# The loop over the batches of an attention and expert block: 28 passes of an engine loop written out as straight code

## The reference, cut to what matters

```python
x = L0_attn_x                                  # [32, 512, 256]
mod = (_silu(L0_c) @ L0_wmod).reshape(32, 6, 1, -1)
sa, ca, ga, sb, cb, gb = (mod[:, n] for n in range(6))
# ga, gb: pushed away from zero to at least 0.25 in size
h = _layernorm(x) * (1 + ca) + sa
x = x + ga * attention(h, w_qkv, b_qkv, w_out, b_out)
#   scores = q.k / 4 + alibi_causal_mask; probs = softmax(scores); out = probs.v @ w_out.T + b_out
h = _layernorm(x) * (1 + cb) + sb
x = x + gb * experts(h, gate_W, expert_W, out_W)
#   p = softmax(h @ gate_W.T); cnt[e] = how many entries of (p > 0.3) equal e; out = sum_e cnt[e] p[e] (h @ expert_W[e].T) @ out_W.T
```

## Time and profile before

| what | us |
|---|---|
| median of 3 runs | 1957.47 |
| fastest and slowest of them | 1957.25, 1957.89 |
| span of the profiled execution, first to last instruction | 1953.2 |
| TensorE busy in it | 1724.6 (88%) |
| VectorE busy | 1552.6 (79%) |
| ScalarE busy | 1214.8 (62%) |
| GpSimd busy | 998.9 (51%) |

### The profile page before, as it was taken

One profiled execution on the slowest core, in us unless ns is written; L12 is line 12 of the kernel. 1 busy time (PEld: TensorE's weight loads), 2 busy tenths in 40 slices (PEclk: granted clock), 3 DMA queues, 4 the chain that ended last, 5 costly groups with the idle time before them and its releaser, 6 DMA issues.

```text
span 1953.2 us, 62334 instructions
## 1 busy us (share of the span) xinstructions
PE 1724.6 (88%) x17744; PEld 995.6 (51%) x17744; DVE 1552.6 (79%) x5632; ACT 1214.8 (62%) x2466; POOL 998.9 (51%) x1225
## 2 busy tenths in 40 slices
PE   5799999998989998999999898999899999999974
PEld 3455555555555455555555555545555555555542
DVE  5778888888888878888888888887888888888843
ACT  1366666666666666666666666666666666666651
POOL 3234555545545455555554554545555545455454
PEclk8799999999999999999999999999999999999986
DMA  4243333433333443333344333344333334433321
GB/s 131 77 133 116 125 119 128 141 128 124 125 104 125 140 136 126 120 125 120 128 141 128 123 125 104 126 141 136 125 120 125 121 129 139 131 123 115 120 88 45
DMA packets 206753, 238.21 MB, mean 122 GB/s; under 512 B 27626, under 2 KB 153138, under 8 KB 206674
## 3 DMA queue, kind: packets, MB, share of 16 engines
q1 hardware_dynamic: 206710, 237.67, 37.3%
HBM read 135.13 MB, written 101.81 MB: 121 GB/s over the span
## 4 chain that ended last, share of the span: by engine, by line
PE 49%; DVE 24%; issue 18%; ACT 4%; DMA 2%; DVEq 2%; POOL 1%; SPq 1%; ACTq 0%; POOLq 0%
PE ps L497 18%; PE ps L589 12%; DVE ps L853 9%; PE ps L575 8%; PE ps L609 4%; PE ps L603 4%; DVE mxt L853 4%; DVE ol L868 2%; DVEq L257 1%; ACT hf_a L658 1%; ACT hh_a L660 1%; DVE qk_st L793 1%; DVE st_c L759 1%; ACT prob L647 1%; PE ps L515 1%
## 5 line engine op out<-in xcount | busy, mean ns | idle before, releaser
L853 DVE CUSTOM_DVE_ANT_0 ps<-ps,mask_qk 128x512 f32<-128x512 f32 (+3 forms) x2048 | 971.1, 510 | 296.3 <-PE ps L589 285.3
L647 ACT ACTIVATE prob<-ps 128x512 f32<-128x512 f32 (+1 forms) x1536 | 743.5, 530 | 363.2 <-PE ps L575 362.3
L589 PE MATMUL ps<-kz,qs 112*128 112x512 f16 (+3 forms) x2048 | 542.4, 307 | 138.2 <-DVE mxt L853 129.5
L1018 POOL TENSOR_SCALAR_AFFINE_SELECT prob<-prob 128x512 f32<-128x512 f32 x512 | 353.4, 696 | 364.2 <-ACT prob L647 364.2
L575 PE MATMUL ps<-qs,kz 114*128 114x128 f16 (+2 forms) x3584 | 453.3, 243 | 3.7 <-DMA qs<-negm 3.1
L589 PEld LDWEIGHTS ps<-kz,qs 112*128 112x128 f16 x2048 | 187.1, 97 | 492.8 <-DVE mxt L853 308.6
L853 DVE DVE_READ_ACCUMULATOR2_ANT mxt<- 128x1 f32 x2048 | 288.6, 141 | 0.0
L575 PEld LDWEIGHTS ps<-qs,kz 114*128 114x128 f16 x3584 | 259.7, 98 | 50.5 <-ACT prob L647 3.8
L609 PE MATMUL ps<-prob,va 128*32 128x384 f32 (+2 forms) x3072 | 237.0, 380 | 0.0
L603 PE MATMUL ps<-prob,va 128*32 128x128 f32 x4096 | 218.3, 285 | 2.0 <-issue 0.9
L679 ACT ACTIVATE qk_st<-ps,bqk 128x512 f16<-128x512 f32 x128 | 88.0, 688 | 97.7 <-PE ps L497 95.7
(11 more groups left out here) (115 smaller groups left out, 2818.7 us busy)
## 6 DMA issues: line engine op xcount, KB each, us to landing
qk_d<-qk_st SPq DMA_DIRECT2D x128, 256.0 KB, 2.0
ou_d<-ou SPq DMA_DIRECT2D x128, 256.0 KB, 2.0
qs<-qk_d SPq DMA_DIRECT2D x128, 192.0 KB, 2.6
kz<-qk_d SPq DMA_DIRECT2D x256, 96.0 KB, 2.6
xa<-in_L_attn_x SPq DMA_DIRECT2D x32, 512.0 KB, 4.3
qk_d<-qk_st SPq DMA_DIRECT2D x128, 128.0 KB, 1.9
xc<-in_L_attn_x SPq DMA_DIRECT2D x32, 512.0 KB, 3.5
oc<-ou_d SPq DMA_DIRECT2D x64, 256.0 KB
```

Source lines behind the costliest of these rows:

```text
L589: x_ = mm(ps[:, bank, col:col + w], qs[0:CONST, h // 2, qt * P:(qt + 1) * P], kz[0:CONST, h, 0:w], start=True, stop=True)
L647: nc.scalar.activation(prob[:, h % 8, at:at + w], ps[:, ST + n, 0:w], ACT.Exp, scale=1.0 / FS).then_inc(s["exp_done"], 1)
L853: x_ = v.tensor_tensor_reduce(ps[:, bank, col:col + w], ps[:, bank, col:col + w], mask_qk[:, S - w:S], 1.0, -3e38, ALU.add, ALU.max, mxt[: ...
L1018: q.affine_select(out=d, in_=d, compare_op=ALU.is_ge, fill=0.0, base=0, pattern=[[0, 4], [1, P]], channel_multiplier=-1).then_inc(s["maske ...
```

## The change

The loop on the engines goes. All 36 iterations are written out with a plain number for i. The order of the work on each engine, the tiles, the tables and the transfers stay.

```diff
         def iterations(eng, one, first=-2):
 
-            for i in range(first, 2):
-                one(i)
-            with eng.Fori(2, NB - 2) as i:
-                one(i)
-            for i in range(NB - 2, NB + 2):
+            for i in range(first, NB + 2):
                 one(i)
```

## The result

The changed kernel took **1899.04 us** (median of 4, 1897.75 to 1901.19), the kernel before 1957.36 beside it; the ratio is 0.970, interval 0.969 to 0.972. The direction was forecast, the size was not: 1923 was said, and 1906 as the low end. The gain is 58 us in place of 34.

What follows compares the result with a forecast made beforehand. TensorE was taken as the bound, waiting 5.2 us per iteration, mostly for VectorE's row maxima. 0.91 + 0.32 = 1.23 us over 28 iterations gave 34.4 us off, hence 1923 us; range 1906 to 1940, 8 in 10.

Steps and rivals of the forecast that it cites:

- The bound and the mechanism: TensorE bounds while fed; its waits for VectorE's maxima shrink as each real hand-over gets 0.16 us shorter, 0.58 to 0.42.
- That hit was on one of the worst places: Late store in iteration 30, delaying the negated maxima, TensorE waiting 0.30 us in slot 8; its net gain taken as mean.
- The 0.91 us: Gain per iteration from head to end of TensorE's longest wait, 45.80 us in iteration 29 against 44.89 in iteration 30.
- The first term: Stretch from iteration head to end of TensorE's longest wait in slot 12: gain of 0.91 us per iteration.
- the second: Rest of the iteration behind the longest wait: 0.92 us less in iteration 30, of which 0.32 credited to the change.
- Iteration 30's missing batch: No batch 32 to load and normalise in iteration 30; the 0.60 us wait behind the statistics was credited to that.
- The low end: Lower end of the 8 in 10 range, 1906 us, the time of the rival giving all 1.83 us to the change.
- Rival 1: Missing statistics cost iteration 30 nothing, so all 1.83 us is the change's: 28 x 1.83 = 51.2, 1906 us; chance 0.12.
- worth of 8 of them: Size check: 1.23 us per iteration equals 8 hand-overs at 0.16 us less each; not a further term.
- Rival 2: Instruction blocks delay transfers more on average than in iteration 30: 1949 us, or 1932 with only 0.32 lost; chance 0.23.
- Rival 3: TensorE runs out of instructions, up to 1.25 us per late block: 2011 us with one in two late; chance 0.05.
- Rival 4: No difference: a wait for DMA in slot 8 or ScalarE takes back the cheaper hand-over, 1957 us; chance 0.05.

Runs made afterwards that it cites:

- e1: All engines written out except TensorE, which keeps the loop of 28 passes: 1880.31 us, ratio 0.960 to the kernel before.

## Why the prediction was wrong

**The bound and the mechanism** were right. TensorE does the same matmuls, and its waits shrank; the hand-over went from 0.58 to 0.42 us as read from the one straight iteration, and putting the increment back brought 0.58 and 36 us. TensorE's own register work and its branch were costed at nothing, and e1 shows it. The clock stayed (a mean of 0.977 to 0.980 in the runs of the kernel before, 0.976 to 0.977 in those of the changed kernel).

**The step that failed** is the one that said of the delayed transfer "That hit was on one of the worst places, so I keep the net figure as the mean over the 28 iterations". The 0.91 us was net of what the late store cost iteration 30, and I had priced that from the one wait marked DMA, 0.30 us. Its true price is seen by iteration 30 of the changed kernel, the same instructions and work: up to the end of the long wait of slot 12 it takes 43.36 us against 44.89, 1.53 less. By slots, 0.91 of it lies in slots 6 to 8 (11.82 against 10.91), 0.34 in the start behind the loop's last pass (2.30 against 2.14 up to the first maximum, and slot 0 4.16 against 3.98), and 0.21 in slot 11, where the pair of `ol` took 2.55 against 2.34 us; no other part is above 0.1. Two more runs bear this out. In e1 only TensorE comes out of a loop ahead of iteration 30, its block starts at 14.6 us, and the stretch takes 44.81. With VectorE alone in the loop TensorE has no block between 10.3 and 22.2 us, and the stretch takes 43.60, although VectorE's start is the slow one. A late transfer also holds ScalarE and the maxima, and such waits bear those engines' names. By the cuts of the prediction:

```
                                before   forecast   mean after   shortest after
head to end of the long wait     45.80     44.89       43.85         43.17
from there to the next head      11.93     11.61       11.78         11.77
sum                              57.73     56.50       55.63         54.95
```

The first term was 1.95 us in place of 0.91, the second 0.15 in place of 0.32. Iteration 30's missing batch was worth 0.77 us (11.01 against 11.78), where I had taken 0.60, the wait alone; that wait is unchanged at 0.60. 28 x 2.10 = 59, where the medians are 58 apart. (The spans of the two profiles are 56.3 apart: iteration 30 gave 1.4 more, and the part ahead of iteration 2, the same code in both, took 3.9 longer in the changed kernel's profile, and why stays open.)

**The low end** failed with it. Rival 1 took 1.83 us as the most that iteration 30 could bear, but a sample that holds a loss is no upper bound of a gain. With the 1.5 us of loss put back the end would have been 1.83 - 0.77 + 1.5 = 2.6 an iteration, 28 x 2.6 = 72 us or 1885, and e1 without TensorE's blocks reaches 1880.

**What the prediction did not see** is the share of GpSimd. It lay inside the 0.91 (slot 11 took 5.38 in iteration 30), but I gave it all to the hand-over, and took "worth of 8 of them" for a check of size. It was a coincidence of sizes.

**The rivals.** Rival 2 (dearer hits on average) was wrong, they are cheaper on average: 0.68 us in the first stretch (43.85 - 43.17), against the 1.3 to 1.45 by which iteration 30 with its block stands above iteration 30 without one (44.89 - 43.60, and 44.81 - 43.36). Rival 3 (TensorE short of instructions) did not come about: no wait for want of instructions grew (0.9 us in all before and after, and a block took 1.1 us, where the rounded share gave 1.25); but slower than before did, in the form of rival 2 and of the lower clock, when TensorE alone was written out. Rival 4 is out. Unlike iterations were forecast, so were 160 and 130 blocks in all: there are 142 and 105. Each 8 KB block holds 128 of the other four engines' 13,477 instructions, and I had extrapolated from a stretch with 5 and 4 blocks, where the average is 4.25 and 3.0. e1 also bears on what the prediction cited on taken branches: TensorE's loop body of some 1,200 instructions runs 28 times there with no 16 KB block after the first pass, in which five start. By that rule of the Trainium skill ("Runtime: NRT & Kernel Launch", Instruction fetch mechanics) each turn of TensorE would have paid for a fetch, and the trace disagrees.

## What to carry to other kernels

A straight iteration next to a loop is a ready-made experiment, but look what fell into it. Here the first block fetches behind the loop put a block beside the same store in one kernel after another. Compare the slots of such an iteration one by one, count the instruction blocks and the landings in it, and take the clean slots for the gain and the disturbed ones for a loss with a frequency of its own. As this kernel has it: unroll an engine for its waits, and leave in the loop an engine whose queue is full anyway, since its code then doesn't compete with short-deadline transfers. Look also at TensorE's clock by iteration and not only as a mean over the run: with TensorE alone written out, a mean of 0.972 in place of 0.977 hid seven iterations of some 3 us more each. An increment or semaphore instruction that holds a wait in front of a work instruction costs its time at every hand-over on the path, even if nobody reads what it counts.

## What the runs showed of the hardware

- A wait held by a semaphore instruction on VectorE in front of the operation made the start 0.16 us later than a wait in the operation, with a constant in both (0.58 against 0.42).
- With a 16 KB block of instructions (about 1.1 us on the DMA engine that carries it) in the same microseconds, a 256 KB store took 3.7 to 4.3 us to land, against 2.2 to 3.0 in the other iterations of the changed kernel. TensorE's blocks cost 19 us here (e1 against the changed kernel). When it alone was written out the median was 21 us longer, a part of it with a lower clock.
- Shortly after waits of TensorE of 0.9 to 2.7 us, or from within them, its clock was at 1.2 GHz for a stretch, in seven of 28 iterations with TensorE alone written out and in ten of 28 with `load_o` moved. Such iterations took 2.7 and 1.6 us more than the others of the same run; how much of that is the wait and how much the clock was not separated.
- TensorE ran a loop body of about 1,200 instructions 28 times, and no 16 KB block was fetched after the first pass.
- Two `ol`, which read `om` and `oh` from SBUF: 1.41 us alone, 2.89 beside a GpSimd addition of 1.27 us and the selects behind it, which took 1.09 us in place of 0.64. Moving the addition by two slots was worth 41 us in the kernel before and 24 us on top of e1, which makes **1856.57 us** the fastest version here.
